# Mode mixing of a spectral convolution: 32 unrolled steps on TensorE, or a loop of two steps fed from fixed buffers

## The reference, cut to what matters

```python
# x (16, 64, 256, 256); weight_re, weight_im (4, 16, 16, 32, 17); all float32
def _L0_conv_ref(x, weight_re, weight_im, bias):
    x_freq = jnp.fft.rfft2(x, axes=(-2, -1))
    xf = x_freq.reshape(B, n_heads, head_in, fH, fW)          # 4 heads of 16 channels
    core = jnp.einsum('bhixy,hioxy->bhoxy', xf[:, :, :, :m_x, :m_y], weight[:, :, :, :m_x, :m_y])
    out_freq = jnp.zeros((B, n_heads, head_out, fH, fW), dtype=core.dtype)
    out_freq = out_freq.at[:, :, :, :m_x, :m_y].set(core)     # m_x = 32, m_y = 17
    x_out = jnp.fft.irfft2(out_freq.reshape(B, n_heads * head_out, fH, fW), s=(H, W), axes=(-2, -1))
    return x_out + bias

x = x + _L0_conv_ref(_gn(x), weight_re, weight_im, bias)      # _gn: group norm, 32 groups of 2 channels
x = x + _L1_conv_ref(_gn(x))                                  # _L1: whitening by a 16x16 covariance
```

## Time and profile before

| | |
|---|---|
| median of 3 runs | 3537.61 us (3537.39 to 3541.55) |
| the profiled execution | 3536.93 us, its span 3535.0 us |
| mode mixing, first matmul to last copy | 175.5 us |
| PE busy in it | 75.7 us, granted clock 0.50 |
| DVE and ACT busy in it | 56.6 and 52.1 us |
| last copy to first matmul of the next stage | 17.5 us |

### The profile page before, as it was taken

One profiled execution on the slowest core, in us unless ns is written; L12 is line 12 of the kernel. 1 busy time (PEld: TensorE's weight loads), 2 busy tenths in 40 slices (PEclk: granted clock), 3 DMA queues, 4 the chain that ended last, 5 costly groups with the idle time before them and its releaser, 6 DMA issues.

```text
span 3535.0 us, 230090 instructions
## 1 busy us (share of the span) xinstructions
PE 2898.4 (82%) x98565; PEld 2038.3 (58%) x98565; DVE 2541.8 (72%) x4358; ACT 1146.3 (32%) x2860; POOL 1116.4 (32%) x1434
## 2 busy tenths in 40 slices
PE   6888888888886342366499999999999999999998
PEld 3555555555554332122377777777777777777776
DVE  4777777777776335755477777777777777777777
ACT  1222222222221221000144444444444444444444
POOL 4666666666665112455111111111111111111111
PEclk8999999999998555799799999999999999999999
DMA  7999999999999761699388888888888888888887
GB/s 229 330 322 331 327 330 323 326 326 327 333 327 274 93 92 19 205 349 352 118 302 302 302 300 301 301 302 300 301 302 301 302 303 300 301 302 302 300 300 279
DMA packets 630257, 1001.81 MB, mean 283 GB/s; under 512 B 103712, under 2 KB 464176, under 8 KB 630192
## 3 DMA queue, kind: packets, MB, share of 16 engines
q1 hardware_dynamic: 528816, 912.44, 78.5%
q10 hardware_dynamic: 101376, 88.39, 8.7%
HBM read 639.40 MB, written 361.28 MB: 283 GB/s over the span
## 4 chain that ended last, share of the span: by engine, by line
PE 50%; issue 15%; ACT 14%; ACTq 10%; DMA 6%; DVE 5%; SPq 0%; DVEq 0%; POOL 0%; POOLq 0%
PE bank L593 15%; ACT reg L645 13%; PE bank L584 11%; ACTq L653 6%; PE bank L421 6%; DMA reg<-xh_d 5%; PE bank L432 5%; PE bank L440 4%; PE bank L454 3%; PE bank L564 2%; PE bank L501 2%; PE bank L525 1%; ACT xh L645 1%; DVE reg L866 1%; PE bank L463 1%
## 5 line engine op out<-in xcount | busy, mean ns | idle before, releaser
L645 ACT ACTIVATE reg<-bank 128x512 f32<-128x512 f32 (+3 forms) x1696 | 844.7, 529 | 1105.7 <-PE bank L593 941.1
L1064 DVE STREAM_TRANSPOSE reg<-bank 128x256 f32<-128x256 f32 x2048 | 738.8, 418 | 335.5 <-PE bank L610 335.5
L768 POOL TENSOR_TENSOR reg<-reg 128x512 f32<-128x512 f32 x512 | 685.9, 1340 | 433.8 <-PE bank L432 402.0
L1068 DVE SCALAR_TENSOR_TENSOR reg<-reg,m,mwhit 128x1024 f32<-128x1024 f32 x512 | 657.8, 1285 | 72.1 <-DVE reg L1064 38.2
L593 PE MATMUL bank<-tab,reg 64*128 64x256 f32 x4096 | 692.5, 404 | 0.0
L822 POOL TENSOR_TENSOR reg<-reg,tab 128x64 f32<-128x64 f32 x512 | 164.2, 321 | 1550.1 <-ACT reg L645 828.0
L854 DVE TENSOR_TENSOR reg<-reg 128x512 f32<-128x512 f32 x512 | 526.5, 1028 | 36.6 <-DVE gmask L872 20.2
L610 PE MATMUL bank<-reg 32*32 32x128 f32 x32768 | 547.0, 279 | 1.7 <-DVE reg L1064 1.7
L610 PEld LDWEIGHTS bank<-reg 32*32 32x32 f32 x32768 | 370.5, 103 | 210.3 <-issue 171.5
L584 PE MATMUL bank<-tab,reg 64*128 64x64 f32 x8704 | 443.5, 235 | 46.2 <-ACT reg L645 46.1
L593 PEld LDWEIGHTS bank<-tab,reg 64*128 64x128 f32 x4096 | 458.5, 187 | 28.0 <-issue 0.7
(11 more groups left out here) (121 smaller groups left out, 1765.2 us busy)
## 6 DMA issues: line engine op xcount, KB each, us to landing
reg<-in_x_dram SPq DMA_DIRECT2D x256, 1024.0 KB, 8.2
reg<-in_x_dram SPq DMA_DIRECT2D x512, 512.0 KB, 3.9
out_dram<-reg SPq DMA_DIRECT2D x512, 512.0 KB, 2.9
xh_d<-xh ACTq DMA_DIRECT2D x128, 512.0 KB
reg<-xh_d SPq DMA_DIRECT2D x128, 512.0 KB, 5.9
gram_d<-gram ACTq DMA_DIRECT2D x64, 256.0 KB
reg<-gram_d SPq DMA_DIRECT2D x64, 256.0 KB, 4.8
spec_d<-psu ACTq DMA_DIRECT2D x512, 8.5 KB
```

Source lines behind the costliest of these rows:

```text
L645: copy = lambda o, i, **k: nc.scalar.activation(o, i, ACT.Copy, **k)
L768: nc.gpsimd.tensor_tensor(out=halves[:, q % 2, 1], in0=x_in[:, 2 * q:2 * q + 2, 0], in1=x_in[:, 2 * q:2 * q + 2, 1], op=ALU.subtract).then ...
L1064: ins = v.transpose(o_sb[:, q].rearrange("p n (f w) -> p f n w", f=2)[:, :, :, BL * j:BL * j + BL], bank[4 + j][:, 0:W].rearrange("p (f n ...
L1068: v.scalar_tensor_tensor(out=o_sb[:, q], in0=o_sb[:, q], scalar=m1[:, ds(t * 4 + q, 1)], in1=mwhit[:, :].unsqueeze(1).to_broadcast([P, 4, W]),
```

## The change

The 32 steps on PE become a loop of 16 trips with two steps in its body. The matmuls read from fixed buffers, two of each kind: `step_w` (weights) and `step_x` (modes). ACT copies each step's weights there with two instructions of 128 x 272 values, the second with the sign as its scale. POOL writes the step's modes, multiplied by the scale, in one instruction of 128 x 272; it also adds the mean, once per head. The step's four row groups write one PSUM bank per part, and DVE alone copies them, two instructions per step over 128 partitions. Ahead of the loop four matmuls fill banks 2 to 5, and each step begins with one `mm` of one column. Every wait in the PE loop is against a count worked out from the loop's register. `msum` and `mwhit` move into `xht`.

```diff
+        steps = sb("steps", [P, 8 * KY * PAIRS])
+        step_w, b = cut(steps, 0, 2, KY, 2, 2, PAIRS)
+        step_x = [a[:, 0:KY * B].rearrange("p (y b) -> p y b", b=B) for a in (flat(gram[:, :, :]), tmp[:, :])]
-        whit, msum, mwhit = sb("whit", [P, 2, P]), sb("msum", [P, 2, P]), sb("mwhit", [P, W])
+        whit, msum = sb("whit", [P, 2, P]), xht[:, 2]
+        mwhit = xht[:, 3].rearrange("p a b -> p (a b)")
...
@@ SP: conv_store; loads of heads 2 and 3
-                sp.wait_ge(*nth("mode_act", h * 2 * KA + KA * (part + 1)))
-                sp.wait_ge(*nth("mode_dve", h * 2 * KA + KA * (part + 1)))
+                sp.wait_ge(*nth("mode_read", h * KA + KA // 2 * (part + 1)))
...
-                    sp.wait_ge(*nth("mode_mm", h * 2 * KA))
+                    sp.wait_ge(*nth("weights_ready", h * KA))
+                    sp.wait_ge(*nth("modes_ready", h * KA))
                     weights_load(h + 1)
                     modes_load(h + 1)
...
@@ TensorE
-            for h in range(HEADS):
-                pe.wait_ge(*nth("modes_ready", h + 1))
-                pe.wait_ge(*nth("weights_ready", h + 1))
-                for a in range(KA):
+            pe.wait_ge(*nth("rot_read", NU))
+            for e in range(4):
+                mm(bank[2 + e][:, 0:32 * 9], T("eye"), tab[:, 0:32 * 9], **one)
+            pe.wait_ge(*nth("rows_ready", 1))
+            with pe.Fori(0, HEADS * KA // 2) as t:
+                for e in range(2):
+                    pe.wait_ge(*nth("weights_ready", t * 2 + e + 1))
+                    pe.wait_ge(*nth("modes_ready", t * 2 + e + 1))
+                    pe.wait_ge(*nth("mode_read", t * 2 + e - 1))
+                    mm(bank[6][:, 0:1], T("eye", 32), tab[0:32, 0:1], **one)
                     for part, (y0, y1) in enumerate(((0, 9), (9, KY))):
-                        n = h * 2 * KA + 2 * a + part
-                        if n >= 2:
-                            pe.wait_ge(*nth("mode_act", n - 1))
-                            pe.wait_ge(*nth("mode_dve", n - 1))
                         for y in range(y0, y1):
                             for g in range(KG):
                                 r = slice(32 * g, 32 * g + 32)
-                                ins = mm(bank[2 * g + part][32 * g:32 * g + B, 32 * (y - y0):32 * (y - y0) + 32],
-                                         modes_in[r, h % 2, :, KY * a + y],
-                                         weights[r, h % 2, :, :, KY * a + y].rearrange("p r (n c) -> p r c n", c=2), **one)
+                                ins = mm(bank[2 + 2 * e + part][32 * g:32 * g + B, 32 * (y - y0):32 * (y - y0) + 32],
+                                         step_x[e][r, y], step_w[r, e, y].rearrange("p r c n -> p (r c n)"), **one)
                         ins.then_inc(S["mode_mm"], 1)
...
@@ ACT
             for h in range(HEADS):
+                act.wait_ge(*nth(f"weights_in{h % 2}", (h // 2 + 1) * (16 * 4 * KG)))
                 for a in range(KA):
+                    n = h * KA + a
+                    if n >= 2:
+                        act.wait_ge(*nth("mode_mm", 2 * n - 2))
+                    for r in range(2):
+                        ins = copy(step_w[:, n % 2, :, r].rearrange("p y c n -> p c n y"),
+                                   weights[:, h % 2, r, :, KY * a:KY * a + KY].rearrange("p (n c) y -> p c n y", c=2),
+                                   **(dict(scale=T("sgn")) if r else {}))
+                    ins.then_inc(S["weights_ready"], 1)
...
@@ GpSimd
-                nc.gpsimd.tensor_scalar(weights[:, h % 2, 1], weights[:, h % 2, 1], T("sgn"), None,
-                                        ALU.mult).then_inc(S["weights_ready"], 1)
...
+                pool.wait_ge(*nth(f"modes_in_in{h % 2}", (h // 2 + 1) * 16 * KG))
+                mi = modes_in[:, h % 2]
+                pch(nc.gpsimd.tensor_tensor(out=mi[:, :, 0], in0=mi[:, :, 0], in1=m0_row[:, h:NU:HEADS], op=ALU.add))
+                for a in range(KA):
+                    n = h * KA + a
+                    if n >= 2:
+                        pool.wait_ge(*nth("mode_mm", 2 * n - 2))
+                    nc.gpsimd.tensor_tensor(out=step_x[n % 2].rearrange("p y b -> p b y"),
+                                            in0=mi[:, :, KY * a:KY * a + KY],
+                                            in1=r0_row[:, h:NU:HEADS].unsqueeze(2).to_broadcast([P, B, KY]),
+                                            op=ALU.mult).then_inc(S["modes_ready"], 1)
...
@@ DVE
+            dve.sem_inc(S["rows_ready"], 1)
             for h in range(HEADS):
                 for a in range(KA):
+                    n = h * KA + a
                     if h >= 1 and a % 4 == 0:
                         dve.wait_ge(*nth(f"conv_stored{a // 4}", h * (16 * KG)))
                     for part, (y0, y1) in enumerate(((0, 9), (9, KY))):
-                        for g in range(2, 4):
-                            ins = v.tensor_copy(modes_out[32 * g:32 * g + B, :, a, :, y0:y1],
...
+                        dve.wait_ge(*nth("mode_mm", 2 * n + part + 1))
+                        ins = v.tensor_copy(modes_out[:, :, a, :, y0:y1],
+                                            bank[2 + 2 * (n % 2) + part][:, 0:32 * (y1 - y0)].rearrange(
+                                                "p (y r n) -> p r n y", r=4, n=PAIRS))
+                    ins.then_inc(S["mode_read"], 1)
```

More of the change, by code:

```diff
@@ L243, in whiten_kernel @@
             spectra_ready stat_mm rot_mm rot_read root_wanted root_done ps_stored
-            modes_in_in0 modes_in_in1 weights_in0 weights_in1 weights_ready modes_ready mode_mm mode_act mode_dve conv_stored0 conv_stored1 conv_in
+            modes_in_in0 modes_in_in1 weights_in0 weights_in1 rows_ready modes_ready weights_ready mode_mm mode_read conv_stored0 conv_stored1 conv_in
             rot2_mm rot2_act c_ready m1_mm var_base var_prod var_ready var_mm r1_ready
@@ L257, in whiten_kernel @@
                                 xh_out1=1, gram_out=1, out_stored0=1, out_stored1=1, out_stored2=1, out_stored3=1),
-                    vector=dict(xt_copied=2, d_copied=1, diag_done=1, rot_read=1, q_read=2),
+                    vector=dict(xt_copied=2, d_copied=1, diag_done=1, rot_read=1, q_read=2, mode_read=2),
                     gpsimd=dict(gram_used=2, w_ready=2))
@@ L770, in _ @@
                                             op=ALU.subtract).then_inc(S["diff_made"], 1)
-            pool.wait_ge(*nth("tab_in", 16))
+            pool.wait_ge(*nth("rows_ready", 1))
             for h in range(HEADS):
-                pool.wait_ge(*nth(f"weights_in{h % 2}", (h // 2 + 1) * (16 * 4 * KG)))
-                nc.gpsimd.tensor_scalar(weights[:, h % 2, 1], weights[:, h % 2, 1], T("sgn"), None,
-                                        ALU.mult).then_inc(S["weights_ready"], 1)
[L777 to L785, removed]
+                pool.wait_ge(*nth(f"modes_in_in{h % 2}", (h // 2 + 1) * 16 * KG))
[9 more added lines that the diff above has]
+                                            op=ALU.mult).then_inc(S["modes_ready"], 1)
             for i in range(NP // VN):
@@ L946, in _ @@
                     for part, (y0, y1) in enumerate(((0, 9), (9, KY))):
-                        dve.wait_ge(*nth("mode_mm", h * 2 * KA + 2 * a + part + 1))
-                        for g in range(2, 4):
-                            ins = v.tensor_copy(modes_out[32 * g:32 * g + B, :, a, :, y0:y1],
-                                                bank[2 * g + part][32 * g:32 * g + B, 0:32 * (y1 - y0)].rearrange(
-                                                    "p (y r n) -> p r n y", r=4, n=PAIRS))
-                        ins.then_inc(S["mode_dve"], 1)
+                        dve.wait_ge(*nth("mode_mm", 2 * n + part + 1))
[3 more added lines that the diff above has]
+                    ins.then_inc(S["mode_read"], 1)
             dve.wait_ge(*nth("conv_in", 16 * 8 * HEADS))
```

## The result

| | before | changed |
|---|---|---|
| median of the runs | 3537.5 us (4 runs, 3534.06 to 3541.55) | 3471.01 us (4 runs, 3469.35 to 3471.51) |
| ratio | | 0.9819, 95% interval 0.9802 to 0.9837 |
| span of the profiled execution | 3535.0 us | 3469.1 us |
| from DVE's copy of the means to the first L510 (now L515) | 214.2 us | 149.1 us |

The change makes the kernel 66.5 us faster. The forecast was 3475, its range 3458 to 3490.

What follows compares the result with a forecast made beforehand. PE waiting for its own code (94.8 us of gaps) was taken to bound the mixing. Its last copy was to end at 1273 instead of 1334.3, 61.3 us off 3536.9, so 3475 us, range 3458 to 3490.

Steps and rivals of the forecast that it cites:

- main forecast: Whole kernel: 3475 us with the mixing's clock still at 0.50, own range 3467 to 3485; chance 0.53.
- first rival: In the mixing: the clock rises, a step takes 1.87 us, 68 us less in all, 3468; chance 0.25.
- The start: Ahead of head 0: without POOL's L775, rows ready about 5.2 us sooner, PE starts at 1154.8 instead of 1158.8.
- The step: PE's loop: 136 matmuls 2.13 us, back edge 0.19, one-column `mm` and waits 0.2; sum 2.5 us a step.
- The back edge: PE's loop: the jump costs 0.37 us a trip, 0.19 a step.
- The first trip's fetch: PE's loop in head 0: fetching the first trip's code takes 2.0 us, bounds 0 and 2.7.
- The feeders: Per step: ACT's copies 0.96 us, POOL's multiply 0.66, DVE's copies 0.89, all under PE's 2.5.
- The loads and SP's queue: Heads 2 and 3: SP's queue takes 36.2 us between their loads; PE waits about 15 us for head 2.
- The wait that becomes late: Head 3: DVE waits for the first half of `conv_store(2)`, landed at 1256.0; the mixing ends at 1273, not 1269.8.
- clock still 0.50: In the mixing: a sign of the forecast, that PE's clock stays at 0.50 as before.
- the four row groups of one bank take turns: PE's matmuls: sharing one bank, they can't run side by side, a step takes 8.5 us; 3630, chance 0.07.
- fetched again at each trip: PE's loop: its code is refetched every trip, 12.7 us a trip, about 25 us slower, 3560; chance 0.02.

Runs made afterwards that it cites:

- x2: The changed kernel with PE's 32 steps written out again instead of the loop; 3533.7 us, 0.9995 of the kernel before.
- x3: The changed kernel with four steps in the loop's body and 8 trips; 3474.5 us, 0.9834 of the kernel before.
- x7: The changed kernel with one extra trip of PE's loop on zeros and old values before head 0; 3466.9 us, 0.9789 of the kernel before.
- x1: The changed kernel run again with no edit; 3470.1 us, 0.9816 of the kernel before.
- x5: The changed kernel with one POOL multiply of head 1's imaginary weights put back beside DVE's statistics; 3480.0 us, 0.9847 of the kernel before.
- x6: The changed kernel without the loads of weights and modes for heads 2 and 3; 3431.2 us, 0.9706 of the kernel before.
- x8: The changed kernel with both head 2 loaded ahead and the extra trip before head 0; 3447.3 us, 0.9735 of the kernel before.
- x4: The changed kernel with head 2's weights and modes loaded ahead into a spare part of the result buffer; 3453.1 us, 0.9767 of the kernel before.

## Why the prediction was right

The forecast put the mixing's end 61.3 us earlier; the stretch is 65.2 us shorter, and the medians differ by 66.5. The mechanism was the one forecast, with one exception: the main forecast kept the clock at 0.50, and it rose in part, as in its first rival. The 3471 us measured lie between that rival's 3468 and the main forecast's 3475. By its own steps, with 3.8 us added to the times of the trace after, so that both have the same origin:

| step | predicted | measured |
|---|---|---|
| first matmul | 1154.8 | 1153.6 |
| load of head 2 issued | 1181.1 | 1180.7 |
| load of head 3 issued | 1217.3 | 1214.5 |
| modes of head 3 used | 1247.6 | 1243.3 |
| DVE's first copy of head 3 | 1256.0 | 1252.7 |
| end of the last copy | 1273 | 1269.3 |
| first matmul after the mixing | 1290.5 | 1286.6 |

*What bounds the kernel.* PE waited for its code. x2 shows it by undoing the loop alone, x3 by the number of gaps, x7 by moving them, and the instruction queue by its 34 packets before and 3 after. By the Trainium skill, "Runtime: NRT & Kernel Launch", instruction fetch mechanics, code comes in blocks of 256 instructions; the counts here agree. The page also holds that the fetch is mostly hidden and that kernels prefer full unrolling. Here the written-out form stands at 0.9995 of the kernel before and the loop at 0.9816, since PE gets through a block in 2.0 us and then stood still for 2.8 us on average.

*The start.* Sized a little small: first matmul 5.2 us sooner (21.3 to 16.1 us after the means) where 4.0 were expected, because head 0's modes were used at 1148.67, 1.7 us after the rows at 1147.0, where 2.7 were taken. That differs from one execution to the next: in x1 they came 2.7 us after the rows, in x3 6.2. The rows themselves were ready at the moment forecast. x5 shows that POOL's instruction did hold DVE.

*The step.* 2.57 us cold against 2.5. The one-column `mm` costs 0.49 us cold and 0.28 warm (L502 to L507), not 0.2; the 136 matmuls take 2.01, not 2.13, which hides part of that. The back edge, the jump to the loop's start, costs 0.2 to 0.5 a trip as taken. The first trip's fetch was 5.0 us, outside its bounds of 0 to 2.7: I had bounded a gap by the shortest one, though a gap of 7.28 stood in the same group. The rise of the clock, at about 1165, gave about as much back in head 0, so that the load of head 2 came within 0.4 us of the forecast. Two errors cancel there, and this was luck of the execution: in x1 the clock did not rise in head 0, and the load came 3.7 us after the forecast's 43.6 us from the means.

*The feeders.* ACT's two copies last 0.67 and 0.72 us, not 0.48, but the second starts 0.48 us after the first (1169.37 and 1168.89), so a step takes 1.2 us; POOL 0.68 (forecast 0.66); DVE 0.46 and 0.42, as on 16 partitions. All stay under the 1.8 of a warm step.

*The loads and SP's queue.* This carried the forecast: saved time goes back in waits for heads 2 and 3. x6 shows it, 41.9 us less of stretch without these loads. The wait that becomes late, DVE for the store of head 2, came as said, and it set the end. SP issued that store at 1242.1 instead of 1246.9, in the times of the table: the queue's period was 33.8 us, not 36.2, and issuing head 3's load took 20.0, not 22.1. From issue to DVE's copy it took 10.6 us, not 9.1. The difference, 3.3 us, is nearly all that the forecast missed. Head 3's load, 28.9 us to the use of its modes and not 30.3, did not set the end.

*The rivals.* The clock did rise, in heads 0 and 1 and at the end of head 2, but not in head 3, which runs at 0.50, so "clock still 0.50" among the signs of the forecast failed; what it saved in head 1 went into the wait for loads, as argued. In x8, where the steps follow one another with fewer waits, the granted clock is 0.74 over the stretch against 0.65. That the four row groups of one bank take turns is refuted: 136 matmuls take 2.01 us at clock 0.50, and took 2.12 before, with a bank for each group. Gotcha 1 of the Trainium skill's "TensorEngine Tiling (Array Packing)" therefore doesn't hold for row groups that also differ in column group; for the same column group no run here shows anything. The body is not fetched again at each trip, with 560 instructions or with 1100.

## What to carry to other kernels

Look for gaps in "issue" at equal counts of instructions: an engine that runs through many short instructions faster than its code arrives is bound by its own code, and then the form of the program, a loop or written out, decides, not its work. Before counting such a gain, ask which transfers the slow engine was hiding; here some 42 us of it went to loads that start only when buffers come free. And a loop still pays for its first trip, more the busier the DMA engines are; an idle stretch ahead of it is the place for that trip.

## What the runs showed of the hardware beyond that

- PE's gaps after 256 instructions were mostly 0.8 to 1.9 us with the DMA engines quiet, 3.5 to 6.5 us beside a load of weights in x2, and 7.0 and 8.7 us in x4 (share 1.24).
- A DVE instruction on 128x64 values took 4.87 us instead of 0.26 beside one POOL instruction on 128x2176. DVE's copies from PSUM were not held: in the kernel before, four of them took 1.83 us from 1160.08 on beside POOL's L784 (1160.04, 3.85 us), 0.46 us each as elsewhere.
- PE on tiles of 32 x 16 can get the full clock, where 75.7 us of the same matmuls broken by gaps had left it at 0.50. Trips without a long gap came before each rise, but not for the same time: about 5 us in head 0 here (from 1160.27), about 10 in x4 and x8, 20.6 in x1. In head 3 here 15.2 us of such trips ended still at 0.50, with PE 98% busy. What decides between these isn't shown.
